# Four edits to a cross-attention and expert kernel: where the output bias is added, when one batch's statistics are taken, which engine makes the slot integers, and products on an idle TensorE

## What is computed

```python
def layer(x, ctx):
    n = layernorm(x)
    q, k, v = n @ Wq.T + bq, ctx @ Wk.T + bk, ctx @ Wv.T + bv      # 16 heads of 16
    a = softmax(q * 0.25 @ k.T) @ v
    x = x + a @ Wo.T + bo                                           # the output bias bo
    n = layernorm(x)
    e = argmax(n @ router_w.T + router_b)                           # one of 32 experts
    return x + relu(relu(n @ weights1[e] + bias1[e]) @ weights2[e] + bias2[e])
```

## Times and profile before

| | us |
|---|---|
| median of 3 runs | 1132.77 |
| lowest, highest | 1130.8, 1137.42 |
| the profiled execution | 1134.33 |
| its span, first to last instruction | 1132.5 |

### The profile page before, as it was taken

How to read it: one execution, slowest core, us unless ns; L and a number is a source line. 1 busy time by engine, 2 the same in 40 slices (tenths; PEclk the granted TensorE clock), 3 DMA queues, 4 the chain that set the end, 5 groups by cost and what they waited for, 6 DMA issues and landing times.

```text
span 1132.5 us, 39071 instructions
## 1 busy us (share of the span) xinstructions
PE 1050.1 (93%) x15015; PEld 877.7 (77%) x15015; DVE 916.1 (81%) x2355; ACT 825.7 (73%) x1892; POOL 839.3 (74%) x1579
## 2 busy tenths in 40 slices
PE   5998999999999999999999999999998369998982
PEld 4887888878888888888888888888886258887872
DVE  4887788888888888888888888888887547776761
ACT  5776787878888888888888888888885236665651
POOL 5436688778878887888888878878866747777776
PEclk9999999999999999999999999999999679999997
DMA  7525222532222222323222222222210366666650
GB/s 234 186 60 130 77 78 77 125 105 77 77 78 82 82 86 78 90 82 104 83 83 77 77 78 77 78 77 78 72 53 22 109 190 200 208 207 210 202 150 12
DMA packets 91164, 120.38 MB, mean 106 GB/s; under 512 B 14105, under 2 KB 73892, under 8 KB 90790
## 3 DMA queue, kind: packets, MB, share of 16 engines
q1 hardware_dynamic: 77159, 84.04, 26.1%
q0 software_dynamic: 13824, 33.85, 8.3%
HBM read 60.61 MB, written 59.31 MB: 106 GB/s over the span
## 4 chain that ended last, share of the span: by engine, by line
PE 80%; DVE 5%; DMA 5%; POOL 4%; issue 3%; ACT 1%; SPq 0%; POOLq 0%; DVEq 0%; ACTq 0%
PE maxima L789 18%; PE pA L849 10%; PE sc L826 10%; PE sc L856 10%; PE sc L796 8%; PE sc L780 5%; PE sc L1036 4%; PE maxima L803 3%; PE maxima L1044 3%; POOL out L431 3%; PE sc L835 2%; DMA arena<-pages 2%; DMA out<-arena 2%; PE sc L1027 2%; PE pA L803 2%
## 5 line engine op out<-in xcount | busy, mean ns | idle before, releaser
L480 ACT ACTIVATE arena<-sc 128x512 f32<-128x512 f32 x512 | 264.4, 603 | 93.3 <-PE sc L835 93.3
L597 DVE TENSOR_REDUCE mx<-maxima 128x4 bf16<-128x512 f32 (+1 forms) x256 | 235.1, 919 | 5.2 <-PE maxima L803 4.0
L431 POOL DMA_INDIRECT out<-arena x160 | 157.6, 985 | 60.3 <-issue 30.8
L396 POOL DMA_INDIRECT pages<-row,slot_i x128 | 130.6, 1020 | 55.4 <-issue 53.4
L826 PE MATMUL sc<-qk 32*128 32x256 f32 x2048 | 152.1, 394 | 0.3 <-DVE xnT L617 0.3
L856 PE MATMUL sc<-wo_s,aT 128*128 128x256 f32 x512 | 132.5, 381 | 7.9 <-ACT arena L480 4.9
L849 PE MATMUL pA<-arena 128*32 128x128 f32 x4096 | 138.4, 276 | 0.0
L622 DVE STREAM_TRANSPOSE tr<-pA 128x512 f32<-128x512 f32 x128 | 90.7, 708 | 43.8 <-PE pA L849 43.4
L557 ACT ACTIVATE arena<-sc 128x256 f32<-128x256 f32 x160 | 61.5, 384 | 79.4 <-PE sc L1027 78.2
L849 PEld LDWEIGHTS pA<-arena 128*32 128x32 f32 x4096 | 107.1, 110 | 10.8 <-issue 5.0
L796 PE MATMUL sc<-wqkv,cHi 128*128 128x256 f32 x512 | 107.3, 302 | 0.0
(11 more groups left out here) (155 smaller groups left out, 2709.8 us busy)
## 6 DMA issues: line engine op xcount, KB each, us to landing
arena<-pages SPq DMA_DIRECT2D x160, 130.0 KB, 3.0
cT<-ctxT SPq DMA_DIRECT2D x64, 256.0 KB, 4.1
xs<-x_in SPq DMA_DIRECT2D x128, 128.0 KB, 3.4
pages<-empty SPq DMA_DIRECT2D x120, 130.0 KB, 3.5
pages<-empty SPq DMA_DIRECT2D x1, 5200.0 KB, 20.0
out<-arena POOLq DMA_INDIRECT x160
w2s<-w SPq DMA_DIRECT2D x1, 2080.0 KB
qk<-w SPq DMA_DIRECT2D x1, 2064.0 KB, 9.9
```

The source lines that it names most:

```text
L396: pool.indirect_dma_start(pages, bass.IndirectOffsetOnAxis(slot_i[:, q % 2, u:u + 1], 0), row[:, q % 4, u, :], None, bounds_check=last_slo ...
L431: pool.indirect_dma_start(out_rows, bass.IndirectOffsetOnAxis(pr[:, r, COL_TOKEN:COL_TOKEN + 1].bitcast(U32), 0), pr[:, r, 0:D], None, bou ...
L480: act.activation(pt[:, u % 2, g].rearrange("p i k -> p (i k)"), sc[g][:, :], ACT.Exp).then_inc(S["exp_out"], 1)
L597: dve.tensor_reduce(mx[:, :].rearrange("p (g h) -> p g h", h=32)[:, g:g + n, 0:4], src.rearrange("p (g h k) -> p g h k", g=n, h=4), AX.X, ...
```

## The change

Four edits, and no other:

1. On GpSimd `add_bo(s)` stands behind `place(s - 3)`, and it waits for `nrm` of the last batch of group s-1 where it waited for the last but one.
2. On VectorE the statistics of the fourth batch are taken in the first step (u=0) of the next stage, between `mxT` and `xnT`, and no longer in the last step (u=3), between `run` and `tr`. The first time (s = -2) stays.
3. The slots become integers on VectorE, right behind their sum, and no longer on GpSimd.
4. TensorE makes seven products of the identity with `wo_s` (each 128x512, float32) into a bank that nobody reads, from the time that the last slots are integers.

```diff
@@ GpSimd
                 if q >= 1:
-                    after(pool, "nrm_out", 4, q - 1, 2)
+                    after(pool, "nrm_out", 4, q - 1, 3)
                 pool.tensor_tensor(xs[:, q % 4], xs[:, q % 4], bo_s[:, :].unsqueeze(1).to_broadcast([P, QB, D]),
@@
-            def slots_as_integers(q):
-                if q >= 2:
-                    scattered(pool, q - 2)
-                after(pool, "slot_out", 1, q, 0)
-                pool.tensor_copy(slot_i[:, q % 2, :], slot[:, :]).then_inc(S["slot_int"], 1)
@@
                 if live(s - 1):
                     rstd2(s - 1, 0)
+                if 0 <= s - 3 < LATE:
+                    place(pool, s - 3)
                 if live(s):
                     add_bo(s)
-                if 0 <= s - 3 < LATE:
-                    place(pool, s - 3)
@@
                 if live(s - 3):
-                    slots_as_integers(s - 3)
                     scatter(s - 3)
@@ VectorE
                 after(dve, "own_slots", 1, q, 0)
-                if q >= 1:
-                    after(dve, "slot_int", 1, q - 1, 0)
                 dve.tensor_reduce(slot[:, :], t1[:, :, :], AX.X, ALU.add).then_inc(S["slot_out"], 1)
+                if q >= 2:
+                    scattered(dve, q - 2)
+                after(dve, "slot_out", 1, q, 0)
+                dve.tensor_copy(slot_i[:, q % 2, :], slot[:, :]).then_inc(S["slot_int"], 1)
@@
                         mxT_copy(qn, un)
+                    if u == 0 and s >= 0 and live(s + 2):
+                        stats1(s + 2, (3,))
                     if u == 3 and live(s + 2):
@@
-                        if u == 3:
+                        if u == 3 and s == -2:
                             stats1(s + 3, (3,))
@@ TensorE
             mid = [mb[0], mb[1], pA, mb[2]]
+            after(pe, "slot_int", 1, NQ - 1, 0)
+            for _ in range(7):
+                pe.matmul(sc[0][:, :], ident, wo_s[:, :, :], start=True, stop=True)
             pe.wait_ge(S["ex_init"], 1)
```

## The result

| | before | changed |
|---|---|---|
| median, us | 1134.7 (6 runs) | 1173.16 (6 runs) |
| lowest, highest | 1130.8, 1137.42 | 1168.82, 1177.57 |
| the profiled execution | 1134.33 | 1175.61 |
| its span | 1132.5 | 1173.7 |

The changed kernel is slower: the ratio is 1.0343, with a 95% interval of 1.0312 to 1.0374. The forecast was 1164, within 1148 to 1176; the median measured lies 9.2 us above the forecast and inside the range.

What follows compares the result with a forecast made beforehand. TensorE's own work was taken as the bound. Collisions of `eq` with `cLo` in 28 stages add 34 us, edits 3 and 4 take 0.5 and 2.4: span 1132.5 to 1163.6, median 1164, range 1148 to 1176.

Steps and rivals of the forecast that it cites:

- The bias behind the places: Edit 1, GpSimd: bias runs from T + 2.4 to T + 4.8, letting VectorE's running sum take about 0.28 us, not 1.07.
- The gain of 0.26 us a stage: Steady stages: TensorE's waiting for VectorE, 26.60 against 26.34 us, removed by edits 1 and 2.
- Statistics, `rs`, `cHi`, `cLo`: Edit 2's chain: statistics end at T + 6.14, `rs` starts T + 6.22, `cHi` T + 8.15, `cLo` T + 11.26.
- the tie that the prediction left open: `nrm` at about T + 8.13 against `cHi` at T + 8.15, unordered; if `nrm` loses it is late by 0.85 us.
- the collision costs more: Rival: `nrm` starts first and holds `cHi` some 0.3 us, so `cLo` ends later; 8.4 us more, 1172; chance 0.12.
- the end of `cLo`: GpSimd, each stage: `cLo` ends at T + 13.65; 0.3 us earlier or later is 8 us to either side.
- The comparison: VectorE's `eq` is held, ending at T + 13.81; TensorE's projection follows 2.22 us later; stage grows 1.31 us.
- The disturbed stages: Stages 2, 7 and 8, already partly disturbed: counted 0.7 us more in stage 2, some 0.5 each in 7 and 8.
- Edit 3: Slot copy moved to VectorE: in the stages inside the sums; at the end saves 0.3 to 0.6 us, taken as 0.5.
- Edit 4: Idle products before the first page raise TensorE's clock: 2.4 us won at the start of the page part.
- the assumption that the clock outlasts this pause: Between the products' end near 912.4 and the first page, the clock stays up, saving 1.7 us on that page's way.
- the clock falls again: Bound of edit 4: clock falls in the 2 us before the page and nothing is won; total 1166 to 1167.

Runs made afterwards that it cites:

- the best order: Changed kernel without the moved statistics, with nine products, `cLo` in two halves around `rs` on GpSimd; 1132.37 us against 1133.8, ratio 0.9992, stages 26.45 us.
- nine products and a pause of 1.48 us: Changed kernel with `cHi` and `cLo` ahead of `rs` on GpSimd, and nine idle products instead of seven; 1143.26 us, ratio 1.0083.
- the table in pieces: Kernel with `cLo` in halves, statistics in the old place and nine products, plus both `w2s` transfers in eight pieces each; 1117.73 us against 1132.6, ratio 0.9873.
- the pieces alone: Kernel before with only the two `w2s` transfers cut in eight pieces each; 1123.48 us, ratio 0.9923.
- both large instructions ahead of `rs`: Changed kernel with `cHi` and `cLo` right behind the bias, ahead of `rs`, on GpSimd; 1145.81 us, ratio 1.0109, stages 27.00 us.

## Why the prediction held, step by step

**The bias behind the places** did what was said. The running sum takes 0.27 us, and the bias runs from 401.37, T + 2.35 with T = 399.02 (forecast T + 2.4), beside no instruction of VectorE with two SBUF inputs.

**The gain of 0.26 us a stage** is there and is used up at once. In the changed kernel the step with the sum takes 6.82 us and not 6.93, but in the next one the later `xnT` takes back more (6.89 for 6.65; see the table). Edit 1 alone wins 0.21 us in these two steps and 0.07 in the whole stage, since `cLo` then touches `eq`; the best order wins 0.15. The term, read from one stage at the end of the loop, was about 0.05 us too large.

**Statistics, `rs`, `cHi`, `cLo`.** Forecast: `rs` at T + 6.22, `cHi` at T + 8.15, `cLo` from T + 11.26. Measured: T + 6.27, T + 8.18 and T + 11.44. The chain of small starts, put together from rows of before, was right to 0.05 us up to `cHi`. Then comes the tie that the prediction left open, `nrm` at T + 8.13 against `cHi` at T + 8.15. It fell out in favour of `nrm` (407.16 against 407.20), and `cHi` took 0.25 us more, of which 0.15 reach `cLo`: it starts 3.26 us behind `cHi`, forecast 3.11. This is the mechanism of the rival "the collision costs more", with 0.15 where it had 0.3. That it is only half of that price is luck of a kind: the forecast could not order the two starts. In the kernel with edit 2 alone the tie went the other way. Its timeline:

```profile
456.27 1.04 POOL L364 CAST cHi<-cT 128x1024 fp32r<-128x1024 f32 x1
...
456.40 1.18 DVE L628 TENSOR_TENSOR nrm<-tr,inv 128x256 f32<-128x256 f32 x1
...
459.45 2.38 POOL L368 TENSOR_TENSOR cLo<-cT,cHi 128x1024 fp32r<-128x1024 f32 x1
```

There `cHi` keeps its 1.04 us and `nrm` pays. But from `rs` to `cLo` are 5.11 us (454.34 to 459.45), where the changed kernel has 5.17 (405.29 to 410.46): who pays at the tie makes 0.06 us for the end of `cLo`. That the stage there is 27.75 and not 28.10 us comes nearly all from the slot copy, as said at that experiment.

**The comparison.** Forecast: it ends 0.16 us behind `cLo`, at T + 13.81, and the projection starts 2.22 us later. Measured: 0.14 us behind, at T + 13.98, and 2.25 us. The loss of a stage is 1.50 us and not 1.31. **The mis-sized term is the end of `cLo`**, by 0.19 us (T + 13.84 for T + 13.65), most of it between `cHi` and `cLo`; over 24 regular stages this is 4.5 us.

By the Trainium skill, page "SBUF — State Buffer", section "SBUF: two separate sides", the two engines' shared port pair is an exclusive lock. That `eq`, `nrm`, the running sum and the slot copy all wait for a GpSimd instruction, and `cHi` for `nrm`, agrees with it. By its letter a held instruction would run its whole length behind the holder; `eq`, 0.29 us long, ends only 0.14 us behind `cLo`.

**The disturbed stages.** The forecast took stages 2, 7 and 8 as partly disturbed. Against the forecast, stage 3 cost 0.8 us more, stage 7 2.7 and stage 8 0.7, stages 0 and 1 0.9, and the start 0.7; the last stages of the loop gave 1.6 back. Stage 7 hangs on the transfer behind `w2s`, which the prediction did not name: it read stages 3 and 7 as given. The place of the old profile that held the most to win was missed.

**Edit 3** was taken at 0.5 us at the end. The scatter starts 0.76 us behind the end of the slot sum where it was 1.09: 0.3 us. What the copy costs in the stages was in the sum for `rs`, but was not named as a price of this edit: with the statistics behind it, 0.27 us a stage. **Edit 4** was taken at 2.4 us and brought 1.0. The products ended as forecast: 2.5 us of pause up to the first page's product (912.4 to 914.91), measured 2.36. The step that failed is the assumption that the clock outlasts this pause. It fell 0.7 us into the first page's products, so that of the 1.7 us on the first page's way 0.3 came; the 0.7 us of the second transfer came in full. The case stands in the prediction as a bound (the clock falls again). With nine products and a pause of 1.48 us 1.5 and 0.7 us were there; with nine and a pause of 2.24 us (the table in pieces) 0.7 and 0.35.

The Trainium skill, page "TensorE: Matmul & The Clock Gate", section "What's actually happening", treats the low clock as what idleness returns to. The rows agree, with a delay: after 2.36 us of pause the clock fell 0.7 us into the new work, and after 1.48 us it stayed.

**Sum.** From the forecast span of 1163.6 to the measured 1173.7 are 10.1 us: 4.5 in the regular stages, 4.2 in stages 3, 7 and 8, 1.6 at the start and in stages 0 and 1, 1.6 at the end, and -1.6 in the last stages make 10.3.

## What stays open

Why TensorE pauses in stage 3, in the midst of a group of products that wait for nothing the trace shows. The row of the kernel before:

```profile
109.68 0.61 PE L803 MATMUL maxima<-qk 32*128 32x128 bf16 x11 [4.24 <-issue]
```

The pause is 2.6 to 5.1 us long in the ten profiles with the table whole, and not always in the same group. It comes with the transfer that clears `w2s` (from 90.2 us on), and it is gone when that comes in pieces. The DMA packets point to the cause. The queue whose kind is "instruction" moves a packet of 16 KB every 7.7 us in the median (130 to 800 us). Between 93 and 107.2 us the kernel before has packets of one queue only, and the one with the pieces alone has two of the other (packets, MB, share of 16 engines):

```profile
q1 hardware_dynamic: 2271, 2.35, 87.6%
```

```profile
q8 instruction: 2, 0.03, 1.1%
```

In all ten profiles TensorE goes on 2.3 to 2.5 us behind the start of the first instruction packet after such a gap, here at 109.68 behind 107.27. So it seems to have run out of instructions that were fetched late beside the 2 MB. Whose instructions a packet holds the trace does not say, and no run tries it by itself. The clock stands at 0.50 from 108.9 to 115.7 us, and this makes the other 2.8 us by which the stage is too long: with both large instructions ahead of `rs` the pause is 2.9 us, the clock does not fall, and stage 3 takes 29.64 us, 2.6 above the others.

Not tried either were edits 2 and 3 without the rest, and an order in which the slot copy meets nothing. In the version of `cLo` in halves that copy takes 0.42 us beside `cHi`, and the step with the slots takes 6.61 us and not 6.55; another 0.05 us a stage above the 26.34 of stage 30 before has no row. What the profiles show of stages 3 and 7 and of the clock at the pages stands on one execution of each kernel.

## What to carry to other kernels

A short instruction that another engine waits for is not free where it stands: ask what starts behind it on the waiting engine, and which instruction of a third queue will then run at the same time. A copy of 0.17 us put ahead of it moved the whole chain by 0.27 us a stage, more than who won a tie between two starts (0.06). Large GpSimd and two-input VectorE instructions in SBUF are to be laid out so that the later one does not want to start inside the other. And before tuning the regular stage by tenths, read the stages that stand out from it: two transfers of 2 MB, cut in pieces, gave 9.1 us, and all the work on the order and the idle products 5.75.

## What was not expected of the hardware

- A transfer of 256 KB issued 1.4 to 2.5 us behind one of 2 MB on the same queue landed after 14.5 to 16.0 us, not 4.1; with the table in pieces and the edits to the order those around the same place took 3.8 to 4.4 us.
- A conversion on VectorE of 4 numbers per partition from fp32 to uint32 in SBUF is held up by GpSimd's copy as the instructions with two inputs are: 0.42 us and not 0.17.
- The loser of a tie between `nrm` and `cHi` pays very different prices: VectorE 0.75 us (1.18 for 0.43), GpSimd 0.25 us (1.29 for 1.04).
- Behind the idle products TensorE's clock stood at 1.00. After pauses of 2.18 to 2.67 us (five profiles, one of them with nine products) it fell to 0.50 only 0.7 to 1.5 us after work had begun again; after pauses of 1.48 and 0.06 us it stayed, and after one of 3.35 us it had fallen before the page.
- Around the start of the transfer that clears 2 MB no instruction packet started for 15 to 17 us, and TensorE went on 2.3 to 2.5 us behind the next one, in all ten profiles.
